# Product-key layer: first queries ahead of the previous norm's last turn, and the down matrix under a semaphore of its own

## What is computed

```
q = (x @ Wq).reshape(b, t, H, 2, DK)                    # H = 4 heads, DK = 64
sim1 = jnp.einsum('bthd,hkd->bthk', q1, keys[:, :, 0, :])   # 128 keys
sim2 = jnp.einsum('bthd,hkd->bthk', q2, keys[:, :, 1, :])
s1, i1 = jax.lax.top_k(sim1, K)                         # K = 8
s2, i2 = jax.lax.top_k(sim2, K)
...
final_scores, pk_idx = jax.lax.top_k(all_scores, K)     # of the 64 sums of a first and a second
...
hidden = jnp.einsum('btd,bthkd->bthk', x, w_down)       # w_down: chosen rows of e_down, 2048 x 256
hidden = jax.nn.silu(hidden)
hidden = hidden * jax.nn.relu(final_scores)
out = jnp.einsum('bthk,bthkd->btd', hidden, w_up)
```

## Time and profile before

| | us |
|---|---|
| median of 3 runs | 2164.84 (2163.73 to 2167.0) |
| the profiled execution | 2162.89 |
| its span in the trace | 2161.1 |
| TensorE busy | 1740.8 (81%) |
| VectorE busy | 1413.3 (65%) |
| ScalarE busy | 833.6 (39%) |

### The profile page before, as it was taken

How to read it: one execution, slowest core, us unless ns; L and a number is a source line. 1 busy time by engine, 2 the same in 40 slices (tenths; PEclk the granted TensorE clock), 3 DMA queues, 4 the chain that set the end, 5 groups by cost and what they waited for, 6 DMA issues and landing times.

```text
span 2161.1 us, 31492 instructions
## 1 busy us (share of the span) xinstructions
PE 1740.8 (81%) x12264; PEld 1270.7 (59%) x12272; DVE 1413.3 (65%) x2572; ACT 833.6 (39%) x1968; POOL 334.7 (15%) x321
## 2 busy tenths in 40 slices
PE   8767678837635777678999969998899997999984
PEld 4445445415412445556777748887788875777751
DVE  7479969779988481535565629998455644455546
ACT  2555430265422106356666622110444433334311
POOL 2235500015500205221122200000000000000002
PEclk9775577855558899989999989999999998999997
DMA  6010020100010301040000020000100203000010
GB/s 131 2 40 1 1 66 6 57 4 1 1 49 1 42 28 55 1 137 1 1 1 1 1 84 1 1 1 1 59 11 4 67 1 101 1 1 1 1 40 20
DMA packets 28062, 55.22 MB, mean 26 GB/s; under 512 B 5590, under 2 KB 21107, under 8 KB 26364
## 3 DMA queue, kind: packets, MB, share of 16 engines
q1 hardware_dynamic: 27916, 53.23, 8.8%
HBM read 45.48 MB, written 1.05 MB: 22 GB/s over the span
## 4 chain that ended last, share of the span: by engine, by line
PE 50%; DVE 17%; issue 5%; ACT 3%; POOL 2%; DMA 2%; SPq 0%; DVEq 0%; POOLq 0%; ACTq 0%
PE banks L1781 8%; PE banks L1764 7%; PE banks L1799 7%; PE banks L1693 6%; DVE big L964 3%; PE banks L2549 3%; PE banks L2562 3%; DVE big L556 2%; PE banks L2585 2%; PE banks L1721 2%; PE banks L464 1%; PE banks L475 1%; PE banks L1738 1%; PE banks L1730 1%; DMA big<-big 1%
## 5 line engine op out<-in xcount | busy, mean ns | idle before, releaser
L1874 DVE TENSOR_REDUCE arena<-banks 128x2 f32<-128x512 f32 x192 | 132.3, 689 | 351.7 <-PE banks L1764 351.7
L2002 ACT ACTIVATE big<-banks,arena 128x256 f32<-128x256 f32 x384 | 190.3, 503 | 119.8 <-DVE arena L1874 99.7
L1764 PE MATMUL banks<-big 128*128 128x256 f32 x768 | 206.8, 393 | 2.9 <-ACT big L2002 2.9
L221 POOL TENSOR_TENSOR ln_rstd<-ln_var_eps,neg_half 128x2 f32<-128x2 f32 x44 | 33.6, 763 | 1131.0 <-DVE ln_var_eps L201 1131.0
L1781 PE MATMUL banks<-big 32*128 32x256 f32 x3072 | 181.6, 383 | 11.2 <-DVE big L1892 10.0
L1799 PE MATMUL banks<-big 128*128 128x256 f32 x768 | 181.2, 381 | 0.3 <-ACT x_feat L247 0.3
L1693 PE MATMUL banks<-x_feat,arena 128*128 128x256 f32 x768 | 176.9, 384 | 0.0
L1781 PEld LDWEIGHTS banks<-big 32*128 32x128 f32 x3072 | 156.6, 186 | 30.8 <-DVE big L1892 12.4
L1764 PEld LDWEIGHTS banks<-big 128*128 128x128 f32 x768 | 137.5, 191 | 45.9 <-issue 32.5
L1799 PEld LDWEIGHTS banks<-big 128*128 128x128 f32 x768 | 144.7, 190 | 28.9 <-issue 9.4
L1693 PEld LDWEIGHTS banks<-x_feat,arena 128*128 128x128 f32 x768 | 148.6, 194 | 22.1 <-issue 1.3
(11 more groups left out here) (353 smaller groups left out, 3054.0 us busy)
## 6 DMA issues: line engine op xcount, KB each, us to landing
big<-big SPq DMA_DIRECT2D x32, 128.0 KB, 6.5
big<-in_ctx_tok SPq DMA_DIRECT2D x8, 512.0 KB, 7.9
arena<-in_L0f_w SPq DMA_DIRECT2D x1, 2048.0 KB, 7.8
arena<-in_L1a_wo SPq DMA_DIRECT2D x1, 2048.0 KB
arena<-in_L1f_gv SPq DMA_DIRECT2D x1, 2048.0 KB
arena<-in_L2a_qk_w SPq DMA_DIRECT2D x1, 2048.0 KB
arena<-in_L2x_q_w SPq DMA_DIRECT2D x1, 2048.0 KB
arena<-in_L2x_kv_w SPq DMA_DIRECT2D x1, 2048.0 KB
```

The lines of the kernel that those rows point to most:

```text
L1764: last = mm(ps[:, h * SEQ:(h + 1) * SEQ], self.q[:, n % 2, r, h * P:(h + 1) * P], k, start=not self.mask, stop=True, skip_group_check=self ...
L1874: ins = v.tensor_reduce(dst, B[4 + u % 2][:].rearrange("p (h k) -> p h k", h=2), AX.X, ALU.max, negate=True)
L2002: last = a(self.probs[:, u % 3, h, :], B[4 + u % 2][:, h * SEQ:(h + 1) * SEQ], ACT.Exp, bias=self.neg_max[:, u % 4, h:h + 1], scale=scale, ...
```

## The change

Seven edits:

1. `down` gets a semaphore of its own, `down_loaded`. The wait for it moves from the start of `ProductKeys.tensor` to just ahead of the first `hidden`. The wait for the rest (`loaded` at 48) stays ahead of the first query.
2. In `big` the tile `q` and the matrix `down` change places: `q` now lies where layer 7 keeps its rows of keys and squares.
3. The first three heads of `queries(0)` on TensorE (`tensor_early`, 6 matmuls, 12 rows in a trace) stand ahead of the last pair's transposes. They wait for `xt_ready` at 30, that is for the first 512 tokens.
4. Their three copies on ScalarE (`scalar_early`) stand ahead of that pair's copy to `x_feat`.
5. Query banks are 0 to 3 for the first half and 6, 7, 0, 1 for the second, in place of 4 to 7 and 6, 7, 6, 7. The waits between the second half's matmuls and their copies go.
6. The wait for the whole of `x_feat` moves behind `similar(0)`.
7. All three `SeqHeads` layers (7, 9, 10) wait on TensorE and ScalarE for the cleared semaphores at their last group; those waits at the norm stay where they were in the code.

```diff
@@ LayerNorm
     def tensor(self, pe):
         if self.ahead:
-            self.ahead.tensor_gates_early(pe)
+            self.ahead.tensor_early(pe)
...
     def scalar(self, act):
+        if self.ahead:
+            self.ahead.scalar_early(act)
         for pair in range(self.first, TILES // 2):
             self.scalar_pair(act, pair)
@@ SeqHeads.tensor (and the same for act in SeqHeads.scalar)
         for n in range(self.n + 2):
             live, ahead = n < self.n, n + 1 < self.n
+            if n == self.n - 1:
+                e.wait_set(pe, self.l + 1)
@@ ProductKeys
+        self.q = big.take(PK_HEADS, TOKENS)
         self.down = big.take(CH, PK_EXPERTS)
-        self.q = big.take(PK_HEADS, TOKENS)
...
-        sp.dma_start(self.down, d[n + "_down"]).then_inc(self.loaded, 16)
+        sp.dma_start(self.down, d[n + "_down"]).then_inc(self.down_loaded, 16)
...
     def q_bank(self, n):
-        return 4 + n if n < PK_HEADS else 6 + n % 2
+        return n if n < PK_HEADS else (n + 2) % 8
+
+    EARLY = 3
+
+    def tensor_queries(self, pe, first, last):
+
+        e = self.e
+        for n in range(first, last):
+            half, h = divmod(n, PK_HEADS)
+            for c in range(CH):
+                ins = e.nc.tensor.matmul(e.bank[self.q_bank(n)][:], self.q_w[:, c, h * P:(h + 1) * P], e.x_feat[:, c, half * BANK:(half + 1) * BANK], start=(c == 0), stop=(c == CH - 1))
+            ins.then_inc(self.q_psum, 1)
+
+    def tensor_early(self, pe):
+        pe.wait_ge(self.loaded, 48)
+        pe.wait_ge(self.e.xt_ready, 4 * (self.l - 1) + 2)
+        self.tensor_queries(pe, 0, self.EARLY)
 
     def tensor(self, pe):
         e, nc, B, mm = self.e, self.e.nc, self.e.bank, self.e.nc.tensor.matmul
-        e.wait_x_feat(pe, self.l)
-        pe.wait_ge(self.loaded, 64)
...
             pe.wait_ge(self.sim_ready, 2 * t + 1 + quarter % 2)
+            if t == 0 and quarter == 0:
+                pe.wait_ge(self.down_loaded, 16)
...
-        queries(0)
+        self.tensor_queries(pe, self.EARLY, PK_HEADS)
         pe.wait_ge(self.q_ready, PK_HEADS)
         similar(0)
-        queries(1)
+        e.wait_x_feat(pe, self.l)
+        self.tensor_queries(pe, PK_HEADS, 2 * PK_HEADS)
...
+    def scalar_early(self, act):
+        self.scalar_queries(act, 0, self.EARLY)
...
-        queries(0)
+        self.scalar_queries(act, self.EARLY, PK_HEADS)
         similar(0)
-        queries(1)
+        self.scalar_queries(act, PK_HEADS, 2 * PK_HEADS)
@@ build
+            if which in (8, 11):
+                blocks[-2][1].ahead = blocks[-1][1]
             scans = which in (1, 4)
             if which == LAYERS[-1]:
-                blocks[-2][1].ahead = blocks[-1][1]
                 continue
```

More of the change, by code:

```diff
@@ L2025, in scalar @@
             live, ahead = n < self.n, n + 1 < self.n
+            if n == self.n - 1:
+                e.wait_set(act, self.l + 1)
             if n:
@@ L2501, in __init__ @@
         self.turned, self.out_done = s(name + "_turned"), s(name + "_out_done")
+        self.down_loaded = s(name + "_down_loaded")
     def sync(self, sp):
@@ L2638, in vector, with scalar_queries @@
             mix(TILES - 1, half)
+    def scalar_queries(self, act, first, last):
+        for n in range(first, last):
+            half, h = divmod(n, PK_HEADS)
+            act.wait_ge(self.q_psum, n + 1)
+            self.e.nc.scalar.activation(self.q[:, h, half * BANK:(half + 1) * BANK], self.e.bank[self.q_bank(n)][:], ACT.Copy).then_inc(self.q_ready, 1)
+    def scalar_early(self, act):
+        self.scalar_queries(act, 0, self.EARLY)
     def scalar(self, act):
         e, B, a = self.e, self.e.bank, self.e.nc.scalar.activation
[L2643 to L2647, removed]
         def similar(t):
@@ L2740, in gates, with tensor_early @@
         last.then_inc(self.gate_psum, 1)
-    def tensor_gates_early(self, pe):
+    def tensor_early(self, pe):
         pe.wait_ge(self.gate_loaded, 16)
@@ L2931, in vector, with scalar_early @@
         shift(3)
+    def scalar_early(self, act):
+        pass
     def scalar(self, act):
```

## The result

| | before | after |
|---|---|---|
| median of the runs | 2165.92 (4 runs, 2163.73 to 2169.30) | 2144.24 (4 runs, 2142.11 to 2146.64) |
| the profiled execution | 2162.89 | 2142.11 |
| its span | 2161.1 | 2140.3 |

The ratio is 0.990 (95% interval 0.9888 to 0.9913): 21.7 us less. Forecast were 16.0 less, and a time of 2146 to 2154. A second set of runs of the same kernel gave 2141.67 against 2165.31, so the excess over the forecast repeats. The median of all eight runs is 2143.3.

The account below looks back on a forecast made before the run. The unbroken chain of waits at the border of layers 7 and 8 (norm, `down` transfer, half-clock queries) was taken as the bound; its terms summed to 16.0 us less, 2164.84 - 16.0 = 2148.8, rounded to 2149.0, range 2146 to 2154.

Parts of the forecast that it names:

- The head: Layer 7's last projection to layer 8's first `hidden`: 32.87 us before, first `hidden` forecast 16.0 us earlier, at 1288.22.
- early heads: Three heads of `queries(0)` ahead of the last pair's transposes: 12 of 16 rows at full clock, 5.15 us.
- transposes: Four transposes of layer 7's last norm pair: 0.44 us on warm TensorE, not 1.10, starting 1.34 later.
- fourth head: Last 4 rows of `queries(0)`, behind the transposes: 1.72 us, ending at 1278.69.
- copy with hand-overs: Between the fourth head and `similar(0)`: 0.02 + 0.61 + 0.04 us, to 1279.36.
- I take 1.00, nearest to the earlier trace: Clock for layer 8's first work: assumed full; if it fell, at most 3.22 us lost, a gain of 12.8.
- "nothing" for TensorE beside a full-rate transfer: In layer 8's head, TensorE working beside the `down` transfer was taken to add no time.
- The loop: Layer 8's eight tiles: both engines enter with their old distance, balance repeats tile for tile, nothing lost.
- the loop gives it back: Rival in layer 8's eight tiles: up to 2 us a tile lost, all of 16.0, about 2165; chance 0.03.
- Only the split works: Rival at layer 8's head: early heads held until the norm ends; gain 7.5, time 2157.3; within a shared 0.11.
- Behind layer 8 every queue has its old order, so the rest of the kernel should move as a block: Everything behind layer 8: no further gain or loss beyond the 16.0 us shift.
- The rule cited: At the first `hidden`: a long moved wait for `down` would cost 3.22 us again; by the sum, no wait.

Follow-up runs that it names:

- e2_early: The changed kernel with the wait for `down` put back ahead of the fourth head, early heads kept; 2162.45 us, ratio 0.9989 to the kernel before.

## Why the prediction was off

*The head* held to 0.02 us: 16.86 for 16.84. Its terms one by one: early heads 5.15 (5.15), transposes 0.44 (0.44), fourth head 1.73 (1.72), copy with hand-overs 0.67 (0.67), `similar(0)` 1.99, `queries(1)` 6.87, no wait for `down`, clock 1.00 throughout. "I take 1.00, nearest to the earlier trace rows" was the right end of that price, and so was "nothing" for TensorE beside a full-rate transfer.

*The loop* held: same period, same waits, the distance of the two engines unchanged. The rival "the loop gives it back" did not come. "Only the split works" did not come either; as an experiment it was mis-sized by 1.3 because I carried 10.09 over to a block that starts after a shorter pause.

*The step that failed* is the sentence "Behind layer 8 every queue has its old order, so the rest of the kernel should move as a block", and with it the range. The order was the old one and the waits were. But the rows of the kernel before show pieces at half clock there (the last turn of layer 8 at 5.36 us where the others take 3.7, the first products of layer 9 at 5.11 where the others take 3.45), and I read the granted clock only around the change. These pieces are on the chain, and the move by 16 us changed which of them lie in half clock. The term that was put at nothing is -1.21 + 1.38 + 1.46 + 1.69 + 0.46 + 0.38 = 4.2 in the traces. With it the forecast of 2148.8 becomes 2144.6, and 2144.24 was measured. I had allowed for the clock in one place, as a loss, and nowhere as a gain. The traces of unfilled kernels now show what a range had to take in: 852.2 to 860.0 us behind the first `hidden`, where it was 856.85, so some 3 to 5 us either way. That it came out as a gain and not as a loss was not forecast, and no row of the kernel before tells its sign.

*The rule cited* from the Trainium skill (page "TensorE: Matmul & The Clock Gate", section "HAM oscillation — how this bites in real kernels": a wait can put the array back to half clock, and each restart is paid) is borne out by e2_early, where the wait for `down` costs a half-clock restart of the fourth head and `similar` (3.79 and 3.78 for 1.73 and 1.99). I applied it to the stretch that I was changing and not to the pauses that stayed.

## What to carry to other kernels

When a change shifts everything behind it, look up the granted clock over the whole rest of the kernel: each block that runs at half clock on the path is a term that can come or go with the shift, and here these terms came to 4.2 of the 20.2 us that the traces show from the change on. Before judging a small edit by its total time, compare the pieces of the chain or fill the other pauses in both kernels; without that, a head 0.45 us shorter looked 4.7 us worse. A split semaphore and work moved into a pause are worth more together (16.0) than apart (8.8 and 3.5), because here the clock stayed up only when neither pause was left.

## What the runs showed of the hardware

The clock granted to TensorE does not fall or rise at a fixed time behind a pause or a start. At the end of layer 9 both kernels have the same pauses of 1.39 and 1.97 us and the same values product behind them, and from 1772 to 1775 that product ran at 1.2 GHz in the one, with TensorE busy 3.00 of 3.00 us, and at 2.4 GHz in the other (1753 to 1756). Between the two the chain's pieces have the same lengths for 240 us ahead of it (the changed kernel stays 18.20 us ahead), so what differed is only when it came. Why the clock fell in the one and not in the other stays open.

The pattern looks in part like a property of the kernel: two executions of the changed kernel, the one with four added matmuls and the one with only the split had 13.7, 3.4, 3.4 and 6.8 us, while a shift of 1.7 us gave another. But it rests on one or two executions of each, and in layer 11 kernels of the same order differed.

Some 90 small matmuls whose results nobody reads, in pauses of TensorE, made the kernel before 12.4 us faster and the changed one 6.7. The fastest kernels here are the filled changed ones, at 2136.6 and 2136.7.

Beside a transfer at 388 GB/s, TensorE was busy for 2.00 of 2.00 us at 2.4 GHz, and `queries(1)` took its old 6.87 us; `down`, moved while TensorE worked at that clock, took its old 7.5 us.
